# Routed rows of 265 words with their first 64 features doubled, in a mixture-of-experts vision layer

## The reference, cut to what matters

```python
pooled = x.reshape(64, 12, 14, 16, 14, 16).sum(axis=(3, 5))         # 196 patches an image
h = einsum('bcij,ce->bije', pooled, channel_weights).reshape(64, 196, 192)
h = h + polynomial_attention(layernorm(h))      # 12 heads, weights relu(1 + qk + qk^2/2), normalised
n = layernorm(h).reshape(12544, 192)
p = softmax(n @ router_w.T)                     # 8 experts
top_w, top_i = top_k(p, 2); top_w = top_w / top_w.sum(-1)
for e in range(8):
    w_e = sum(top_w * (top_i == e))
    out = out + w_e * (gelu(n @ w1[e] + b1[e]) @ w2[e] + b2[e])      # 192 -> 768 -> 192
result = h + out
```

## Time and profile before

| | us |
|---|---|
| three runs | 1279.28, 1280.63, 1282.81 |
| median | 1280.63 |
| profiled execution, its own time | 1280.55 |
| its span | 1278.7 |
| granted TensorE clock, mean over the span | 0.952 |
| TensorE busy | 1195.3 |
| VectorE busy | 883.1 |
| ScalarE busy | 598.6 |
| GpSimd busy | 557.9 |

### The profile page before, as it was taken

How to read it: one execution, slowest core, us unless ns; L and a number is a source line. 1 busy time by engine, 2 the same in 40 slices (tenths; PEclk the granted TensorE clock), 3 DMA queues, 4 the chain that set the end, 5 groups by cost and what they waited for, 6 DMA issues and landing times.

```text
span 1278.7 us, 25861 instructions
## 1 busy us (share of the span) xinstructions
PE 1195.3 (93%) x7219; PEld 1073.0 (84%) x7219; DVE 883.1 (69%) x2860; ACT 598.6 (47%) x1143; POOL 557.9 (44%) x453
## 2 busy tenths in 40 slices
PE   5868766999999999999999999999999999999996
PEld 3766655989888898989888888898989899999996
DVE  6788888787878787969697878787845223223443
ACT  0222224454645454546454645454555445454564
POOL 0104433325454545463636363636373753443533
PEclk9986566999999999999999999999999999999998
DMA  9788988778888888797979797979453854454555
GB/s 352 243 294 332 334 311 280 248 233 253 248 257 251 259 238 272 231 277 224 283 215 295 211 295 213 293 214 293 107 134 79 252 117 108 91 105 97 105 138 117
DMA packets 124823, 284.41 MB, mean 222 GB/s; under 512 B 23091, under 2 KB 68772, under 8 KB 124772
## 3 DMA queue, kind: packets, MB, share of 16 engines
q1 hardware_dynamic: 82570, 241.95, 56.4%
q0 software_dynamic: 41568, 41.24, 18.5%
q10 hardware_dynamic: 634, 0.61, 0.2%
HBM read 228.79 MB, written 54.95 MB: 222 GB/s over the span
## 4 chain that ended last, share of the span: by engine, by line
PE 73%; DVE 15%; issue 5%; ACT 3%; DMA 2%; SPq 1%; POOL 0%; ACTq 0%; DVEq 0%; POOLq 0%
PE ps L1003 25%; PE ps L972 21%; PE ps L812 6%; PE ps L919 4%; PE ps L943 3%; PE ps L944 3%; PE ps L908 3%; PE ps L898 2%; DVE red L1084 2%; PE ps L886 2%; DVE red L1081 1%; DVE topi L1220 1%; PE ps L876 1%; PE ps L1001 1%; DMA w1r<-L_attn_w_qkv 1%
## 5 line engine op out<-in xcount | busy, mean ns | idle before, releaser
L629 POOL DMA_INDIRECT result<-ys,ridx x210 | 331.7, 1580 | 305.1 <-ACT ys L770 164.4
L1003 PE MATMUL ps<-w2a,hid 128*128 x2520 | 457.5, 327 | 0.0
L1003 PEld LDWEIGHTS ps<-w2a,hid 128*128 128x128 f32 x2520 | 416.1, 190 | 11.7 <-issue 0.2
L614 POOL DMA_INDIRECT rows_d<-rows,sloti x224 | 217.7, 972 | 363.3 <-ACT rows L726 299.9
L737 ACT ACTIVATE hid<-ps,b1s 128x512 f32<-128x512 f32 (+1 forms) x344 | 222.9, 654 | 233.3 <-PE ps L972 222.9
L1084 DVE TENSOR_REDUCE red<-xbuf 128x21 f32<-128x672 f32 x344 | 279.0, 842 | 4.8 <-PE ps L876 2.4
L972 PE MATMUL ps<-xh,w1h 128*128 128x512 f32 (+1 forms) x344 | 163.6, 476 | 7.2 <-DVE xb L1329 7.1
L1340 DVE TENSOR_TENSOR w1l<-w1r,w1h 128x768 fp32r<-128x768 f32 x116 | 110.5, 953 | 81.1 <-ACT w1h L749 80.4
L972 PE MATMUL ps<-xb,w1h 128*128 128x512 f32 (+1 forms) x344 | 130.1, 378 | 0.0
L972 PE MATMUL ps<-xh,w1l 128*128 128x512 f32 (+1 forms) x344 | 130.1, 378 | 0.0
L972 PE MATMUL ps<-xl,w1h 128*128 128x512 f32 (+1 forms) x344 | 129.9, 378 | 0.0
(11 more groups left out here) (162 smaller groups left out, 1557.9 us busy)
## 6 DMA issues: line engine op xcount, KB each, us to landing
xbuf<-x SPq DMA_DIRECT2D x224, 672.0 KB, 6.2
w1r<-L_ffn_w SPq DMA_DIRECT2D x118, 384.0 KB, 4.8
xr<-rows_d SPq DMA_DIRECT2D x48, 402.0 KB, 3.9
result<-h1s SPq DMA_DIRECT2D x16, 588.0 KB, 7.4
w2a<-L_ffn_w SPq DMA_DIRECT2D x8, 576.0 KB, 7.0
rows_d<-pad SPq DMA_DIRECT2D x9, 402.0 KB, 4.4
rows_d<-rows,sloti POOLq DMA_INDIRECT x224
result<-ys,ridx POOLq DMA_INDIRECT x210
```

The lines of the kernel that those rows point to most:

```text
L614: pool.indirect_dma_start(rows_d, bass.IndirectOffsetOnAxis(ap=sloti[:, k * RT + t:k * RT + t + 1], axis=0), rows[:, t, :], None).then_inc ...
L629: pool.indirect_dma_start(out, bass.IndirectOffsetOnAxis(ap=ridx[:, b, n:n + 1], axis=0), ys[:, b, n, :], None, compute_op=ALU.add).then_i ...
L1003: last = mm(yout(g, b, n), hid[:, m % 3, cols], w, start=False, stop=m == MC - 1 and n % 2 == 1)
```

## The change

A row gets 265 words: after its number (now at word `ID` = 200) come its features 0 to 63 once more. VectorE writes them in two parts, `D.0` for the first four row tiles and `D.1` for the other three, and the scatters wait for these instead of for ScalarE's rows. X0 now turns features 64 to 191. The last 64 words of one group's row and the first 64 of the next group's are neighbours in `xr`, so X1 takes these 128 words and turns features 0 to 63 of two groups by one product: two products for four groups, one for two. Its result has even groups on partitions 0 to 63 and odd ones on 64 to 127, so ScalarE's copy and VectorE's subtraction become two halves each, with the high part of a group on the partitions where it was turned and the low part on the others. w1's rows are permuted on the host to match. `attA` shares its SBUF with `gws`, `attB` with `us`.

```diff
-ROW = E + NE + 1
+ID = E + NE
+ROW = ID + 1 + E - 128
@@ STEP_ALONE, ORDER[2], LAST
-    T1 S10 T2 R V.0 V.1 S11 V.2 V.3 S9 Q0 Q1 Q2 Q3""".split()
+    T1 S10 T2 R V.0 V.1 S11 V.2 V.3 S9 D.0 D.1 Q0 Q1 Q2 Q3""".split()
-    """M0 P <N4 <N5 <Y M1 M2 V.0 S11 S9 <I W0 V.1 V.2 N0 P X0 Z0 V.3 M3 N1 N2 P X1 W1 M4
+    """M0 P <N4 <N5 <Y M1 M2 V.0 S11 S9 <I W0 V.1 V.2 N0 P X0 Z0 D.0 V.3 M3 N1 N2 P X1 D.1 W1 M4
        I P L B Z1 P P M5 <F Q0 Q1 Q2 Q3 <A""".split(),
-    R V.0 S11 V.1 V.2 S9 V.3 Q0 Q1 Q2 Q3 P P P G2 P P P P G3 P P P P""".split()
+    R V.0 S11 V.1 V.2 S9 V.3 D.0 D.1 Q0 Q1 Q2 Q3 P P P G2 P P P P G3 P P P P""".split()
@@ SBUF
-        gws = sb("gws", [NF, IPS, NV])
-        us = sb("us", [NF, HEADS, IPS, HV])
+        first_half = sb("products_or_turned_a", [KA, max(IPS * NV, NT * TOK)])
+        second_half = sb("weights_or_turned_b", [KB, max(IPS * NV, NT * TOK)])
...
+        attA, attB = first_half[:, 0:NT * TOK], second_half[:, 0:NT * TOK]
@@ where X1's groups lie
+        def last_rows(t, half, nb, g, odd):
+            return t[half * KB1:(half + 1) * KB1, nb, 0:128 * g].rearrange(
+                "p (a o r) -> p a o r", o=2, r=128)[:, :, odd]
+        def turned_rows(b, odd, g):
+            return ps[odd * KB1:(odd + 1) * KB1, bank(b, "X1"), 0:64 * g].rearrange("p (a r) -> p a r", r=128)
@@ GpSimd, Q
-                wait_first(pool, s_norm, s * 4 + q + 1)
+                wait_first(pool, s_twice, s * 2 + q // 2 + 1)
@@ ScalarE, X1
-                    copy(xb[KB1:128, nb, 0:128 * g], ps[KB1:128, bank(b, "X1"), 0:128 * g]).then_inc(s_xa, 1)
+                    for o in range(2):
+                        last = copy(last_rows(xb, o, nb, g, o), turned_rows(b, o, g))
+                    last.then_inc(s_xa, 1)
@@ TensorE, X
-                for n in range(groups(j + 1)):
-                    last = turn(ps[:, bank(b, f"X{q}"), n * 128:(n + 1) * 128], xr[:, nb, n, q * KB1:q * KB1 + 128])
+                if q == 0:
+                    for n in range(groups(j + 1)):
+                        last = turn(ps[:, bank(b, "X0"), n * 128:(n + 1) * 128], xr[:, nb, n, KB1:E])
+                else:
+                    for n in range(0, groups(j + 1), 2):
+                        both = xr[:, nb].rearrange("p n c -> p (n c)")[:, n * ROW + ID + 1:(n + 1) * ROW + KB1]
+                        last = turn(ps[:, bank(b, "X1"), n * 64:n * 64 + 128], both)
@@ VectorE, X1 and the new D
-                    V.tensor_tensor(xb[0:KB1, nb, 0:128 * g], ps[KB1:128, bank(b, "X1"), 0:128 * g],
-                                    xb[KB1:128, nb, 0:128 * g].bitcast(F32), ALU.subtract).then_inc(s_xd, 1)
+                    for o in range(2):
+                        last = V.tensor_tensor(last_rows(xb, 1 - o, nb, g, o), turned_rows(b, o, g),
+                                               last_rows(xb, o, nb, g, o).bitcast(F32), ALU.subtract)
+                    last.then_inc(s_xd, 1)
+            def D(s, h):
+                dve.wait_ge(s_norm, s * 4 + 2 * h + 2)
+                some = slice(4 * h, min(4 * h + 4, RT))
+                V.tensor_copy(rows[:, some, ID + 1:ROW], rows[:, some, 0:KB1]).then_inc(s_twice, 1)
@@ host
-            a = np.concatenate([a, a[:, 128:]], 1).reshape(NE, 2, 128, 2, HF).transpose(0, 2, 3, 1, 4).reshape(NE, 128, 2 * FF)
+            a = np.concatenate([a[:, KB1:], a[:, :KB1], a[:, :KB1]], 1).reshape(NE, 2, 128, 2, HF).transpose(0, 2, 3, 1, 4).reshape(NE, 128, 2 * FF)
```

More of the change, by code:

```diff
@@ L223, in vit_layer @@
         phiT = sb("phiT", [NF, NT * TOK])
-        gws = sb("gws", [NF, IPS, NV])
-        us = sb("us", [NF, HEADS, IPS, HV])
+        first_half = sb("products_or_turned_a", [KA, max(IPS * NV, NT * TOK)])
+        second_half = sb("weights_or_turned_b", [KB, max(IPS * NV, NT * TOK)])
+        gws = first_half[0:NF, 0:IPS * NV].rearrange("p (i v) -> p i v", i=IPS)
+        us = second_half[0:NF, 0:IPS * NV].rearrange("p (h i v) -> p h i v", h=HEADS, i=IPS)
+        attA, attB = first_half[:, 0:NT * TOK], second_half[:, 0:NT * TOK]
         rden = sb("rden", [TOK, 2, HEADS])
         att = sb("att", [TOK, NT, ATT])
-        attA = sb("attA", [KA, NT * TOK])
-        attB = sb("attB", [KB, NT * TOK])
         h1s = sb("h1s", [RP, RT, RES])
@@ L348, in vit_layer @@
         s_gap, s_th, s_norm = sem("gap_ready"), sem("tanh_ready"), sem("rows_normalised")
+        s_twice = sem("first_features_twice")
         s_mask, s_rank = sem("mask_ready"), sem("rank_ready")
@@ L604, in _ @@
             set_wait(pool, "pool", "zeros")
-            given("pool", "pad", nc.gpsimd.tensor_copy(pad[:, :, ROW - 1:ROW].bitcast(I32), padi[:].unsqueeze(2)))
+            given("pool", "pad", nc.gpsimd.tensor_copy(pad[:, :, ID:ID + 1].bitcast(I32), padi[:].unsqueeze(2)))
             def Q(s, q):
-                wait_first(pool, s_norm, s * 4 + q + 1)
+                wait_first(pool, s_twice, s * 2 + q // 2 + 1)
                 if q == 0:
@@ L1246, in S11 @@
                     dve.wait_ge(d_scat, s * (32 * RT))
-                mark(V.tensor_copy(rows[:, :, ROW - 1:ROW].bitcast(I32), ids[:].unsqueeze(2)))
+                mark(V.tensor_copy(rows[:, :, ID:ID + 1].bitcast(I32), ids[:].unsqueeze(2)))
                 own(s)
@@ L1346, in I @@
                 g = groups(j + 1)
-                V.tensor_reduce(ridx[:, nb, 0:g], xr[:, nb, 0:g, ROW - 1:ROW].bitcast(I32), AX.X,
+                V.tensor_reduce(ridx[:, nb, 0:g], xr[:, nb, 0:g, ID:ID + 1].bitcast(I32), AX.X,
                                 ALU.max).then_inc(s_idx, 1)
@@ L1401, in _ @@
             schedule(dve, {"P": P_left, "S1": S1, "S2": S2, "T2": T2, "S6": S6, "S8": S8, "S10": S10, "R": R,
-                           "S11": S11, "S9": S9, "L": L, "X": X, "I": I, "Z": Z, "G0": G0, "G1": G1, "G2": G2},
+                           "S11": S11, "S9": S9, "D": D, "L": L, "X": X, "I": I, "Z": Z, "G0": G0, "G1": G1, "G2": G2},
                      before_tail=list_ends)
```

## The result

Six runs of each: 1290.54 us (1289.75 to 1293.08) against 1280.21 (1279.28 to 1282.81), a ratio of 1.0078 with a 95% interval of 1.0066 to 1.0089: 10 us slower. The forecast was 1286.1 in a range of 1278.5 to 1291.5, slower the likeliest. The profiled execution took 1291.99 us, span 1290.2.

The account below looks back on a forecast made before the run. VectorE was taken to set the pace for 28.8 of a loop step's 64.86 us, TensorE for the other 36 and the tail. -3.5 + 1.8 + 3.6 + 3.7 = +5.6 us on 1280.55 gave 1286.1, range 1278.5 to 1291.5.

Parts of the forecast that it names:

- Part 1, products: X1 on TensorE: 0.11 us per product saved; tail -3.5 us, loop step -0.22 and -0.2 us.
- In the tail nothing else limits: Tail: TensorE alone sets the pace, so eleven four-group and ten two-group tiles gain 3.5 us.
- Part 5: Joint before the tail: wider rows cost 3.3 us in pad writes and 0.4 in the load, +3.7 us (0.5 to 5).
- Part 2, halves: X1's subtraction on VectorE in two halves: 0.91 us against 0.72, +0.19; ScalarE's longer copies cost nothing.
- the rule: VectorE: an instruction starting in another partition quarter waits for its predecessor's end; without it the sum is 2.6 us lower.
- Part 3, doubling in the loop: VectorE's stretch in the loop: D.0 +0.20 us a step, D.1 nothing; loop in all +0.16 a step, +1.8 us.
- Part 3, steps alone: Four steps at the start: D.1 waits for ScalarE's rows and delays the pooling, together +3.6 us (2 to 4.5).
- The absorption: Steps alone: VectorE's idle time takes part of the 1.4 us delay, leaving +0.8, +0.8 and +0.6 us.
- Part 4, GpSimd's queue: Q0 waits for D.0, about 2 us later; costs nothing unless the landing slips by more than 9 us.
- Pads hidden: Rival at the joint: SyncE's issues set the pace, wider packets fit between; 3.3 us go, 1282.8 us; chance 0.22.
- The products' time passes: Rival in the loop: VectorE's stretch is no bound, a step loses three times 0.22 us; 1277.1 us; chance 0.13.
- Transfers bind: Rival: later, wider scatters push tile 1's adds, 0.3 us a step, plus 1.9 of lower clock; 1291.3 us; chance 0.10.

Follow-up runs that it names:

- the last experiment: Changed kernel with SyncE's row load ahead of the w1 load in the middle tile of each three in the tail: 1290.03 us, ratio 1.0064.
- the pads later: Pad writes four and four behind the tail's first two row loads, their landing wait moved too: kernel before 1276.77 us, changed kernel 1286.04 us.

## Why the prediction was right, and where its steps were not

Direction and range held; the middle was 4 us low, and the result lies only 1.0 us inside the range. Part of that is luck: by the table's rows 8.2 us were forecast too low and 2.3 too high, which cancel in part. By parts, forecast against the ratios of the runs: wider rows +3.7 against +6.0, X1 -3.9 against -2.3, doubling +5.8 against +6.3. X1 was to be worth more than the wider rows cost, and was worth less than half of it.

- **Part 1, products.** Right in the full tail: 1.93 us over ten tiles for 2.1, that is 0.20 in each of nine where I had 0.22. In the halved tiles the products' 0.11 us do show (7.12 to 7.01, 9.33 to 9.24), and are lost again: this term of the sum, -1.0 of the 3.5, had the wrong sign, +3.7 in the profile after and +0.6 or more in every profile with wide rows but the last experiment's. The +3.7 is a high one: the ten profiles with wide rows have 76.8 us on average and the three with narrow rows 74.7, so +2.1. The step that failed is "In the tail nothing else limits", and Part 5 with it, which gives the loads a price at the joint alone: I read the earlier trace rows, which are full tiles, for the halved ones too, where a tile lasts 7 to 9 us instead of 13 to 19 and its load comes behind w1.
- **Part 2, halves.** Right, with the rule: 0.86 + 0.03 for 0.72, +0.17 where I had +0.19. ScalarE's longer copies cost nothing, as costed.
- **Part 3, doubling in the loop.** D.0 +0.20 in the timeline, 0.22 by its removal. The step grew by 0.02 us and not by 0.16, because X1 gave more than I let it: without the doubling a step is 0.20 shorter than before. From tile 1's xl to tile 0's first product the stretch is 607.95 - 578.91 = 29.04 us for 28.79, so +0.25 where the sum had +0.38: the two pairs of halves cost 0.17 each for 0.19, and the gaps gave back 0.29 for 0.2. That is the 1.4 us by which the ten steps were forecast too long.
- **Part 3, steps alone.** The mechanism was right, down to the 1.4 us by which the pooling is late. The absorption was mis-sized: I let idle time take 0.6 to 0.8 of it. From ScalarE's first rows to the first expert product eight profiles without the doubling on VectorE take 118.8 to 120.8 us, mean 119.7, and six with it 124.4 to 125.6, mean 125.3: 5.5 us, that is 1.2, 1.2 and 1.8 for the three steps and 1.3 behind the last. Almost nothing absorbs it, and in the third step more comes than the 1.4 that I took as the most. The profile after, +4.44, is the lowest of the six.
- **Part 4, GpSimd's queue.** Right in the loop: the scatters start 2.7 us later where I had 2, and TensorE has no wait for the adds there. In the last step the lateness is real and hidden by the pads, as the pads later showed.
- **Part 5, rows.** The right place, mis-sized. The wait grew by 5.5 us: 4.1 from the pads where I had 3.3, 0.6 from the load for 0.4, and 0.7 because TensorE came to the wait that much sooner after the first pad's issue (15.8 us for 16.5). That the load stands behind a wait for the landing, and not only behind the issues, is in the program and not in my account. The lower clock behind it, which I kept out of the sum as an extra of up to 1.9, took about 1.2.
- **Rivals.** Pads hidden fell: with 1.05 MB more, issues and landing both stretched. The products' time passes fell: TensorE's wait for xb grew from 0.16 to 0.52 us a step, and every 0.2 us taken from the stretch came off the step (64.88 to 64.66). Of Transfers bind the lower clock came, at 1.2 us for its 1.9, and the adds' wait only once the pads were out of the way.

What would show it, in turn: steps of 65.0 (64.88) and a wait of 0.8 (0.52) were near, D.1's wait of over 1 us was 0.92, tail tiles 0.20 shorter for 0.22, the joint 7.69 for 6.

## What to carry to other kernels

Before an engine's busy time is traded for bytes, look where the bytes stand in line: here 0.22 us a tile of TensorE time was bought with a third more bytes in every row, and much of the price was paid at the one place where the program makes a load wait until bulk writes have landed. A tail of smaller tiles has other limits than the tiles before it and needs rows of its own. A copy that waits for another engine costs the wait for all that stands behind it in its queue: put it on the engine that would wait anyway, and look at what the other engines execute meanwhile.

## What the runs showed that I had not expected

Beside a 0.40 us copy on GpSimd a VectorE addition of two SBUF operands took 0.42 us for 0.22, and a pooling reduction its usual 0.84. Pad writes that are moved ahead of an earlier load hold that one up instead (2.21 us became 2.16, 7.69 became 5.92); moved behind the load, with the wait for their landing, they cost the kernel before nothing that shows (tile 37 at 18.54 us). And the start differs by 2 us between profiles before any D has run: ScalarE's first rows start anywhere from 93.91 to 96.00 us in the fourteen profiles.
